# Softmax reciprocal moved from VectorE to GpSimd, with the sum of exponentials placed one product earlier

## Chip, cores and metric

One core of one Trainium2 chip runs the whole kernel. The metric is the device time of one execution in microseconds, the median of several runs. The batch is 8 images of 64 channels and 64 x 64 pixels, in float32.

## What is computed

The reference is an attention layer followed by three residual convolution steps. The attention is unusual: it runs over the batch. For each pixel (4096 of them), the 8 images are the 8 tokens, and 8 heads of 8 channels attend among them. Cut to what matters here:

```
xn = group_norm(x); t = xn @ ciw + pe; tn = layer_norm(t)
q2, k2, v2 = projections of tn, as (image, pixel, head, 8)
scores = einsum('inhd,jnhd->nhij', q2, k2) / sqrt(8)
attn = softmax(scores, axis=-1)          # over the 8 images j
z = einsum('nhij,jnhd->inhd', attn, v2)
t = z @ wout + t;  t = gated_mlp(layer_norm(t), t) + t;  x = t @ cow + x
for _ in range(3): x = x + conv(relu(conv(x, w1) + b1), w2) / 3
out = relu(x)
```

The change touches only the denominator of the softmax.

## The kernel before

**Stages.** `setup_weights` folds the weights and computes the group statistics. `attention_block` walks over 32 tiles (`TILES`) of 128 pixels. `conv_steps` does the convolutions. The change is in `attention_block` alone.

**A tile.** Pixels lie on the 128 partitions. A tile's q, k and v are 64 values per image and pixel. The products q.k of all image pairs and heads are made on VectorE (DVE) as four instructions of 1024 elements per partition each (`dve_p1`, b = 0 to 3, line 516). TensorE (PE) sums them over the 8 channels of a head with eight accumulating transposes for each of the four (line 558), ScalarE (ACT) copies the transposed scores out of PSUM (line 718), and PE transposes them back (line 567). DVE takes the maximum (line 770) and subtracts it (line 781), ACT makes the exponential (line 722), DVE sums over the images into `den`, 128 x 64 (`dve_sum`, line 787), takes the reciprocal into `rden` (`dve_reciprocal`, line 793) and multiplies (`dve_attn`, line 799). Four products attn.v (`dve_p2`, line 526) follow, which PE sums (line 577). Then come the output projection (line 587), the residual `z1` (`dve_z1`, line 813), the second normalization (`tn2`, line 825) and the gated MLP (`gated`, line 839).

**The order of the work.** Each engine has one in-order instruction stream. It is written out by hand in `pe_iteration`, `act_iteration`, `dve_iteration` and `pool_iteration`; iteration t works on up to five tiles at once, t to t - 4. A wait is on a semaphore that another engine's instruction raises; an engine that waits holds back all that stands behind. One iteration of DVE has 21 instructions, among them `sum` of tile t - 2, `var1` of tile t (line 755), `reciprocal` and `attn` of tile t - 2.

**GpSimd (POOL) before the change** has three instructions in an iteration: `pool_rstd2` of tile t - 4, `pool_bias` of tile t - 1 and `pool_rstd1` of tile t. The two `rstd` (lines 900 and 907) take an 8-element variance to the power of -0.5 with a tensor_tensor whose operation is `pow` and whose second operand is a constant tile. `pool_bias` (line 760) adds the q and k biases, 1024 elements per partition. `rstd1` of a tile releases `act_scale` in the next iteration (8 ACTIVATEs, line 713), that releases `pool_bias`, and that the first product `dve_p1(t, 0)`.

```
rstd1 (POOL, iteration t) -> act_scale -> pool_bias (iteration t+1) -> dve_p1 b=0 (end of t+1)
exp (ACT) -> sum -> reciprocal -> attn -> p2 b=0..3 (DVE)
```

Of the kernel before, what the change touches and what calls it, by code (L numbers as in the profile page):

```python
# [12 lines left out]
B, C, HW = 8, 64, 64  # L13
# [7 lines left out]
P = 2 * C  # L21
# [8 lines left out]
ALU, ACT, AX = mybir.AluOpType, mybir.ActivationFunctionType, mybir.AxisListType  # L30
# [4 lines left out]
def wait(eng, sem, n):  # L35

    if isinstance(n, int) and n <= 0:
        return
    eng.wait_ge(sem, n)
# [377 lines left out]
def attention_block(nc, d, top):  # L417


    with ExitStack() as ctx:  # L420
        def sb(name, shape, dt=F32):
            return ctx.enter_context(nc.sbuf_tensor(name, shape, dt))

        def sem(name):
            return ctx.enter_context(nc.semaphore(name))
# [22 lines left out]
        exps = shifted  # L448
        den = sb("den", [P, C])
        rden = sb("rden", [P, C])  # L450
        attn = sb("attn", [P, S])
        z = sb("z", [P, N])
        z1 = [sb(f"z1_{k}", [P, N]) for k in range(2)]
# [30 lines left out]
        den_done, rden_done, biased, p1_dve = sem("den_done"), sem("rden_done"), sem("biased"), sem("p1_dve")  # L484
        p2_dve, tn2_done, var2_done = sem("p2_dve"), sem("tn2_done"), sem("var2_done")
        gated_done, x_done = [sem(f"gated_done{e}") for e in range(2)], [sem(f"x_done{e}") for e in range(2)]
        rstd1_done, rstd2_done, attn_done, rrep_done = sem("rstd1_done"), sem("rstd2_done"), sem("attn_done"), sem("rrep_done")

        ident, center = top["consts"][:, K_ID:K_ID + P], top["consts"][:, K_CEN:K_CEN + P]
# [261 lines left out]
        def dve_var1(dve, t):  # L751
            for g in range(2):
                wait(dve, squares_out[g], t + 1)
            wait(dve, rstd1_done, t)
            dve.tensor_scalar(var1[:, :], sumsq[:, :], 1e-5, None, ALU.add).then_inc(var1_done, 1)  # L755

        def pool_bias(pool, t, k):
            wait(pool, scaled_out, B * (t + 1))
            qk = qkv[k][:, :, 0:2 * C]
            pool.tensor_tensor(qk, qk, top["brep"][:, :].unsqueeze(1).broadcast_to([P, B, 2 * C]), ALU.add).then_inc(biased, 1)  # L760

        def dve_p1(dve, t, k, b):
            wait(dve, biased, t + 1)
            wait(dve, scoresT_mm, DUOS * (t - 1) + b + 1)
            p1_product(dve, k, b).then_inc(p1_dve, 1)

        def dve_max(dve, t):
            wait(dve, scores_mm, t + 1)
            wait(dve, shift_done, t)
            dve.tensor_reduce(smax[:, :].rearrange("p (i h) -> p i h", i=B), scores_view(), AX.X, ALU.max).then_inc(smax_done, 1)  # L770
# [5 lines left out]
        def dve_shift(dve, t):  # L776
            wait(dve, scores_mm, t + 1)
            wait(dve, smax_done, t + 1)
            wait(dve, attn_done, t)
            top_of = smax[:, :].rearrange("p (i h) -> p i h", i=B).unsqueeze(3).broadcast_to([P, B, HEADS, B])  # L780
            dve.tensor_tensor(shifted[:, :].rearrange("p (i h j) -> p i h j", i=B, j=B), scores_view(), top_of, ALU.subtract)\
                .then_inc(shift_done, 1)

        def dve_sum(dve, t):
            wait(dve, exp_out, t + 1)
            wait(dve, rden_done, t)
            dve.tensor_reduce(den[:, :].rearrange("p (i h) -> p i h", i=B),
                              exps[:, :].rearrange("p (i h j) -> p i h j", i=B, j=B), AX.X, ALU.add).then_inc(den_done, 1)

        def dve_reciprocal(dve, t):  # L790
            wait(dve, den_done, t + 1)
            wait(dve, attn_done, t)
            dve.reciprocal(rden[:, :], den[:, :]).then_inc(rden_done, 1)

        def dve_attn(dve, t):
            wait(dve, rden_done, t + 1)
            wait(dve, p2_dve, DUOS * t)
            r = rden[:, :].unsqueeze(2).broadcast_to([P, C, B])
            dve.tensor_tensor(attn[:, :].rearrange("p (g j) -> p g j", j=B),
                              exps[:, :].rearrange("p (g j) -> p g j", j=B), r, ALU.mult).then_inc(attn_done, 1)  # L800

        def dve_p2(dve, t, k, b):
            wait(dve, attn_done, t + 1)
            wait(dve, av_mm, DUOS * (t - 1) + b + 1)
            p2_product(dve, k, b).then_inc(p2_dve, 1)
# [10 lines left out]
        def dve_var2(dve, t):  # L816
            wait(dve, var2_mm, t + 1)
            wait(dve, rstd2_done, t)
            dve.tensor_scalar(var2[:, :], b4[:, 0:B], 1e-5, None, ALU.add).then_inc(var2_done, 1)  # L819
# [9 lines left out]
        def of_half(buffer, e):  # L829

            return buffer[:, :].rearrange("p (d e n) -> p e d n", d=2, e=2)[:, e]

        def dve_gated(dve, t, e):

            wait(dve, a_mm, 2 * t + e + 1)
            for d in range(2):
                wait(dve, gelu_out[d], t + 1)
                wait(dve, out_mm[d], t)
            dve.scalar_tensor_tensor(of_half(gated, e), (b5, b7)[e][:, :].rearrange("p (d n) -> p d n", d=2), cols[:, 2:3],
                                     of_half(gel, e), ALU.add, ALU.mult).then_inc(gated_done[e], 1)  # L840
            if t == TILES - 2 and e == 0:
                outer_ahead(dve, ((0, 0), (0, 1), (1, 0)))
            if t == TILES - 1 and e == 0:
                outer_ahead(dve, ((0, 2), (1, 2)))
# [13 lines left out]
        def dve_x(dve, t, k, d):  # L858

            if isinstance(t, int):  # L860
                dve.wait_ge(xr_in[k % 2], 32 * (t // 2 + 1))
            else:
                dve.wait_ge(xr_in[k % 2], (t - k % 2) * 16 + 32)
            wait(dve, cow_mm, t + 1)
            dve.scalar_tensor_tensor(x_view(t, d), x_psum(d), cols[:, 4:5], xr_view(k, d), ALU.add, ALU.add).then_inc(x_done[d], 1)
# [17 lines left out]
        def outer_ahead(dve, pieces):  # L883
            for i, c in pieces:
                free_for(dve, i)
                written(dve, c)
                mix_outer(dve, top["mixed_x"][i], top["outer_done"][i], c, x_piece(i, c))
# [111 lines left out]
        def dve_iteration(dve, t, k, tiles):  # L999
            if tiles[1]:  # L1000
                dve_p1(dve, t - 1, (k - 1) % RING, 1)
            if tiles[4]:
                dve_gated(dve, t - 4, 1)
                dve_gated(dve, t - 4, 0)
            if tiles[1]:
                dve_p1(dve, t - 1, (k - 1) % RING, 2)
            if tiles[2]:
                dve_sum(dve, t - 2)
            if tiles[0]:
                dve_var1(dve, t)  # L1010
            if tiles[1]:
                dve_p1(dve, t - 1, (k - 1) % RING, 3)
            if tiles[2]:
                dve_reciprocal(dve, t - 2)
                dve_attn(dve, t - 2)
                dve_p2(dve, t - 2, (k - 2) % RING, 0)
            if tiles[3]:
                dve_var2(dve, t - 3)
            if tiles[2]:
                dve_p2(dve, t - 2, (k - 2) % RING, 1)  # L1020
                dve_p2(dve, t - 2, (k - 2) % RING, 2)
            if tiles[4]:
                dve_x(dve, t - 4, (k - 4) % RING, 1)
            if tiles[2]:
                dve_p2(dve, t - 2, (k - 2) % RING, 3)
            if tiles[1]:
                dve_max(dve, t - 1)
                dve_shift(dve, t - 1)
            if tiles[4]:
                dve_x(dve, t - 4, (k - 4) % RING, 0)  # L1030
            if tiles[3]:
                dve_tn2(dve, t - 3)
            if tiles[0]:
                dve_p1(dve, t, k, 0)
            if tiles[2]:
                dve_z1(dve, t - 2, (k - 2) % RING)

        def pool_iteration(pool, t, k, tiles):
            if tiles[4]:
                pool_rstd2(pool, t - 4)  # L1040
            if tiles[1]:
                pool_bias(pool, t - 1, (k - 1) % RING)
            if tiles[0]:
                pool_rstd1(pool, t)

# [6 lines left out]
        def run(eng, iteration):  # L1052

            for t in range(TILES + 5 - 1):
                iteration(eng, t, t % RING, [0 <= t - s < TILES for s in range(5)])
# [3 lines left out]
        @block.tensor  # L1059
        def _(pe):  # L1060
            run(pe, pe_iteration)
# [10 lines left out]

        @block.gpsimd
        def _(pool):
            run(pool, pool_iteration)

        @block.sync
# [451 lines left out]
```

## Time and profile before

| | us |
|---|---|
| median of 3 runs | 1140.54 (1140.28 to 1140.69) |
| span of the profiled execution | 1136.3 |
| PE busy | 1071.2 (94%) |
| DVE busy | 1039.7 (92%) |
| ACT busy | 652.5 (57%) |
| POOL busy | 510.7 (45%) |

The run of the profile has no time of its own apart from its span; the span counts from the first to the last instruction and lies 4.2 us under the median of the runs. Setup ends at about 44.6 us, the attention pipeline is full from about 95 to 565 us and drains until about 600 us, and the rest is convolution. PE's ends are modelled, so 94% does not say that PE is at its peak.

### The profile page before, as it was taken

What the parts mean: (1) busy time and instruction counts of PE and PEld (TensorE: products, weight loads), DVE (VectorE), ACT (ScalarE), POOL (GpSimd) and SP (SyncE); (2) the same over time, 40 slices, a digit from 0 to 9 for tenths busy, and PEclk for the clock granted to TensorE, in tenths of its full rate; (3) what the DMA queues carried; (4) which work ended last, traced back from release to release, by engine and by line L of the source; (5) the groups of instructions that cost most, each with busy time, mean ns of one, the idle gap of its engine ahead of it and who ended that gap; (6) DMA issues with size and microseconds to landing.
All of it is one profiled execution on the core that took longest, in us unless ns stands there. A gap on an engine that the chain in (4) does not pass through costs nothing. (4 is left out here: it accounts for less than half of the span.)

```text
span 1136.3 us, 21019 instructions
## 1 busy us (share of the span) xinstructions
PE 1071.2 (94%) x7238; PEld 601.7 (53%) x7238; DVE 1039.7 (92%) x1475; ACT 652.5 (57%) x1525; POOL 510.7 (45%) x422
## 2 busy tenths in 40 slices
PE   4269999999999999999999999999999999999996
PEld 3156787778777777777653333333333333333331
DVE  5459999999999999999988999999999999999996
ACT  4568889888888888888743233253244242342333
POOL 5134564456445544554452424435345344444440
PEclk9999999999999999999999999999999999999998
DMA  8110111111111111110000000030001100030003
GB/s 303 54 37 21 39 29 35 32 39 29 33 35 38 29 31 38 38 29 20 20 20 1 1 1 1 1 75 1 1 1 34 41 1 1 1 74 1 1 1 74
DMA packets 87545, 35.83 MB, mean 32 GB/s; under 512 B 70210, under 2 KB 86851, under 8 KB 86931
## 3 DMA queue, kind: packets, MB, share of 16 engines
q1 hardware_dynamic: 85634, 33.81, 11.1%
q8 instruction: 61, 1.00, 0.4%
q0 software_dynamic: 768, 0.33, 0.2%
q10 hardware_dynamic: 1040, 0.35, 0.1%
q14 instruction: 42, 0.34, 0.1%
HBM read 26.09 MB, written 8.39 MB: 30 GB/s over the span
## 5 line engine op out<-in xcount | busy, mean ns | idle before, releaser
L1173 ACT ACTIVATE y<-banks,cols 128x1024 f32<-128x1024 f32 x96 | 110.3, 1208 | 259.8 <-PE banks L1165 259.8
L900 POOL TENSOR_TENSOR rstd<-var,half 128x8 f32<-128x8 f32 x32 | 80.8, 2526 | 216.5 <-DVE var L755 216.5
L1155 PE MATMUL banks<-mixed_h,cwp 128*128 128x512 f32 x384 | 177.6, 605 | 0.0
L1155 PE MATMUL banks<-early,cwp 128*128 128x512 f32 x372 | 169.2, 602 | 0.5 <-PEq L420 0.5
L1456 POOL TENSOR_TENSOR early<-xs 128x256 f32<-128x256 f32 x95 | 77.1, 811 | 160.1 <-DVE xs L1204 160.1
L1181 DVE TENSOR_TENSOR y<-y,banks 128x512 f32<-128x512 f32 x192 | 119.9, 682 | 15.2 <-ACT y L1173 15.0
L558 PE MATMUL banks<-consts,early 128*128 128x128 f32 x1024 | 133.2, 279 | 0.0
L1189 DVE TENSOR_TENSOR y<-y,banks 128x512 f32<-128x512 f32 x192 | 124.4, 685 | 8.7 <-PE banks L1165 6.5
L577 PE MATMUL banks<-consts,prod 128*128 128x128 f32 x1024 | 128.2, 273 | 2.8 <-DVE prod L526 2.1
L1155 PEld LDWEIGHTS banks<-mixed_h,cwp 128*128 128x128 f32 x384 | 69.0, 189 | 107.9 <-issue 107.9
L558 PEld LDWEIGHTS banks<-consts,early 128*128 128x128 f32 x1024 | 114.3, 144 | 18.8 <-issue 18.1
L516 DVE TENSOR_TENSOR early<-early 128x1024 f32<-128x1024 f32 x96 | 116.6, 1219 | 7.4 <-POOL early L760 7.1
L1155 PEld LDWEIGHTS banks<-early,cwp 128*128 128x128 f32 x372 | 67.7, 190 | 101.4 <-issue 88.8
L526 DVE TENSOR_TENSOR prod<-attn,early 128x1024 f32<-128x1024 f32 x96 | 116.7, 1241 | 0.8
L577 PEld LDWEIGHTS banks<-consts,prod 128*128 128x128 f32 x1024 | 114.6, 141 | 4.5 <-DVE prod L526 3.4
L1196 ACT ACTIVATE h<-y 128x512 f32<-128x512 f32 x96 | 55.0, 625 | 90.2 <-DVE y L1189 89.3
L907 POOL TENSOR_TENSOR rstd<-var,half 128x8 f32<-128x8 f32 x32 | 80.6, 2520 | 53.7 <-DVE var L819 53.7
L1456 POOL TENSOR_TENSOR mixed_h<-h 128x256 f32<-128x256 f32 x48 | 37.5, 781 | 127.4 <-ACT h L1196 127.4
L1165 PE MATMUL banks<-mixed_h,cwp 64*64 64x512 f32 x768 | 93.5, 602 | 0.0
L1165 PE MATMUL banks<-early,cwp 64*64 64x512 f32 x768 | 90.7, 598 | 0.0
L547 PE MATMUL banks<-basis,tt 64*128 64x256 f32 x512 | 76.4, 418 | 11.3 <-ACT tt L688 5.9
L1449 DVE TENSOR_TENSOR early<-xs 128x512 f32<-128x512 f32 x96 | 83.7, 912 | 0.8
(184 smaller groups left out, 1868.8 us busy)
## 6 DMA issues: line engine op xcount, KB each, us to landing
xs<-in_x SPq DMA_DIRECT2D x4, 2048.0 KB, 16.5
xa<-in_x SPq DMA_DIRECT2D x32, 256.0 KB, 2.8
xr<-in_x SPq DMA_DIRECT2D x64, 128.0 KB, 2.8
out_y<-xs SPq DMA_DIRECT2D x32, 256.0 KB, 4.5
cw<-in_L_conv_w POOLq DMA_DIRECT2D x2, 144.0 KB, 3.9
consts<-in_consts ACTq DMA_DIRECT2D x1, 192.0 KB
group<-in_consts SPq DMA_DIRECT2D x1, 64.0 KB
w1n<-in_L_conv_w ACTq DMA_DIRECT2D x1, 64.0 KB
```

What stands on the lines that cost most here:

```text
L516: return eng.tensor_tensor(out, q, kk, ALU.mult)
L526: return eng.tensor_tensor(out, a, v, ALU.mult)
L558: m = pe.matmul(b2[:, P * b:P * (b + 1)], prod1[:, e, P * b:P * (b + 1)], ident, start=(e == 0), stop=(e == HD - 1), is_transpose=True)
L577: m = pe.matmul(b4[:, TILE * p:TILE * (p + 1)], prod2[:, j, P * p:P * (p + 1)], ident, start=(j == 0 and p == 0), stop=(j == B - 1 and p = ...
L900: pool.tensor_tensor(rstd1[:, :], var1[:, :], top["half"][:, :], ALU.pow).then_inc(rstd1_done, 1)
L1155: pe.matmul(psum[PSUM_PAIR[v, q, j]][i][:, :, :], weights(v, i, j).rearrange("p n o -> p (n o)"), mixed[v][i][:, s0:s0 + WIDE, j, :], star ...
L1165: m = pe.matmul(psum[PSUM_PAIR[v, q, j]][i][out, :, :], edge_weights(v, i, j)[rows, :], mixed[v][i][rows, s0 + near:s0 + near + WIDE, j, : ...
L1173: act.activation(pairs(y[i][q][:, :, :]), m1, ACT.Identity, bias=cols[:, (6, 8)[v]:(7, 9)[v]]).then_inc(m1_out[i][q], 1)
L1181: m = dve.tensor_tensor(even_odd, even_odd, psum[PSUM_PAIR[v, q, 3]][i][:, :, :], op)
L1189: dve.tensor_tensor(even_odd, even_odd, psum[PSUM_PAIR[v, q, j]][i][:, :, :], ALU.add).then_inc(y_done[i][q][j], 1)
L1449: eng.tensor_tensor(r, column_pairs(x[:, :, 0:HW]), column_pairs(x[:, :, 2:2 + HW]), ALU.subtract).then_inc(done[c], 1)
L1456: eng.tensor_tensor(r[:, :, 2, :], even_odd[:, 0], even_odd[:, 1], ALU.add)
```

## The change

`reciprocal` leaves DVE. POOL makes the same value as `den` to the power of -1 with a tensor_tensor of 64 elements per partition, against a constant tile `minus` filled once with -1.0. The new instruction stands in POOL's order between `pool_bias` and `pool_rstd1`. On DVE `sum` moves ahead of the third product, so that the third product (b = 2), `var1` and the fourth product (b = 3) stand between `sum` and `attn`.

```diff
+        minus = sb("minus", [P, C])
...
-        def dve_reciprocal(dve, t):
-            wait(dve, den_done, t + 1)
-            wait(dve, attn_done, t)
-            dve.reciprocal(rden[:, :], den[:, :]).then_inc(rden_done, 1)
+        def pool_reciprocal(pool, t):
+            wait(pool, den_done, t + 1)
+            wait(pool, attn_done, t)
+            if t == 0:
+                wait(pool, minus_set, 1)
+            pool.tensor_tensor(rden[:, :], den[:, :], minus[:, :], ALU.pow).then_inc(rden_done, 1)
...
+            if tiles[2]:
+                dve_sum(dve, t - 2)
             if tiles[1]:
                 dve_p1(dve, t - 1, (k - 1) % RING, 2)
-            if tiles[2]:
-                dve_sum(dve, t - 2)
             if tiles[0]:
                 dve_var1(dve, t)
             if tiles[1]:
                 dve_p1(dve, t - 1, (k - 1) % RING, 3)
             if tiles[2]:
-                dve_reciprocal(dve, t - 2)
                 dve_attn(dve, t - 2)
...
             if tiles[1]:
                 pool_bias(pool, t - 1, (k - 1) % RING)
+            if tiles[2]:
+                pool_reciprocal(pool, t - 2)
             if tiles[0]:
                 pool_rstd1(pool, t)
...
+            pool.memset(minus[:, :], -1.0).then_inc(minus_set, 1)
```

DVE's order in the middle of an iteration in the kernel before (early is the buffer of the q.k products, qkv a ring buffer of q, k and v):

```order
L516 TENSOR_TENSOR early<-qkv 128x16x8x8
L787 TENSOR_REDUCE den<-shifted 128x64
L755 TENSOR_SCALAR var<-sumsq 128x8
L516 TENSOR_TENSOR early<-qkv 128x16x8x8
L793 RECIPROCAL rden<-den 128x64
L799 TENSOR_TENSOR attn<-shifted,rden 128x512
L526 TENSOR_TENSOR prod<-attn,early 128x1024
```

The same place with the change, where the line numbers are a few higher:

```order
L789 TENSOR_REDUCE den<-shifted 128x64
L518 TENSOR_TENSOR early<-qkv 128x16x8x8
L757 TENSOR_SCALAR var<-sumsq 128x8
L518 TENSOR_TENSOR early<-qkv 128x16x8x8
L803 TENSOR_TENSOR attn<-shifted,rden 128x512
L528 TENSOR_TENSOR prod<-attn,early 128x1024
```

`den` is ready one product earlier, and DVE has one instruction fewer per iteration. POOL's order before, one and a half iterations:

```order
L760 TENSOR_TENSOR qkv<-qkv,brep 128x8x128
L900 TENSOR_TENSOR rstd<-var,half 128x8
L907 TENSOR_TENSOR rstd<-var,half 128x8
L760 TENSOR_TENSOR early<-early,brep 128x8x128
L900 TENSOR_TENSOR rstd<-var,half 128x8
```

And with the change, with what each waits for:

```order
L762 TENSOR_TENSOR qkv<-qkv,brep 128x8x128 [waits scaled_out]
L797 TENSOR_TENSOR rden<-den,minus 128x64 [waits attn_done,den_done]
L904 TENSOR_TENSOR rstd<-var,half 128x8 [waits scaled_out,var1_done]
L911 TENSOR_TENSOR rstd<-var,half 128x8 [waits rrep_done,var2_done]
L762 TENSOR_TENSOR early<-early,brep 128x8x128 [waits scaled_out]
```

`rstd1` (L900, now L904) and everything behind it on POOL now stands behind the 64-element `pow`.

## Rows read from the trace of the kernel before

**Rows 1.** Busy time by stretch, whole core; the row of the full attention pipeline.
```profile
core 0: us, PE busy (x) PEld busy (x) DVE busy (x) ACT busy (x) POOL busy (x), PEclk, DMA share, GB/s
95.00:565.00 470.00, 468.39 (x4362) 355.77 (x4361) 457.40 (x607) 408.75 (x1140) 246.28 (x87) 1.00 0.13 32
```

**Rows 2.** Timeline, one iteration of DVE: start, duration, engine, line.
```profile
300.13 1.22 DVE L516 TENSOR_TENSOR early<-qkv 128x1024 f32<-128x1024 f32 x1
301.62 0.75 DVE L813 SCALAR_TENSOR_TENSOR z<-banks,cols,tt 128x512 f32<-128x512 f32 x1 [0.27 <-PE banks L587]
...
304.74 1.22 DVE L516 TENSOR_TENSOR early<-qkv 128x1024 f32<-128x1024 f32 x1
305.87 0.68 DVE L787 TENSOR_REDUCE den<-shifted 128x64 f32<-128x512 f32 x1
306.47 0.17 DVE L755 TENSOR_SCALAR var<-sumsq 128x8 f32<-128x8 f32 x1
306.57 1.23 DVE L516 TENSOR_TENSOR early<-qkv 128x1024 f32<-128x1024 f32 x1
307.71 0.55 DVE L793 RECIPROCAL rden<-den 128x64 f32<-128x64 f32 x1
308.29 0.69 DVE L799 TENSOR_TENSOR attn<-shifted,rden 128x512 f32<-128x512 f32 x1
309.02 1.22 DVE L526 TENSOR_TENSOR prod<-attn,early 128x1024 f32<-128x1024 f32 x1
310.24 2.35 DVE L526 TENSOR_TENSOR prod<-attn,early 128x1024 f32<-128x1024 f32 x2
314.04 0.68 DVE L770 TENSOR_REDUCE smax<-banks 128x64 f32<-128x512 f32 x1
316.41 1.22 DVE L516 TENSOR_TENSOR early<-early 128x1024 f32<-128x1024 f32 x1
```

**Rows 3.** Timeline of POOL in the same iteration.
```profile
306.71 2.58 POOL L900 TENSOR_TENSOR rstd<-var,half 128x8 f32<-128x8 f32 x1 [6.64 <-DVE var L755]
310.40 2.55 POOL L907 TENSOR_TENSOR rstd<-var,half 128x8 f32<-128x8 f32 x1 [1.10 <-DVE var L819]
312.92 3.44 POOL L760 TENSOR_TENSOR early<-early,brep 128x1024 f32<-128x1024 f32 x1
```

**Rows 4.** POOL's power instructions of 4 and 8 elements while DVE holds nothing up.
```profile
40.66 1.04 POOL L346 TENSOR_TENSOR ga<-gvar,gexp 128x4 f32<-128x4 f32 x1 [9.59 <-DVE gvar L296]
...
54.10 1.64 POOL L900 TENSOR_TENSOR rstd<-var,half 128x8 f32<-128x8 f32 x1 [12.40 <-DVE var L755]
...
209.03 1.65 POOL L900 TENSOR_TENSOR rstd<-var,half 128x8 f32<-128x8 f32 x1 [6.64 <-DVE var L755]
```

**Rows 5.** Timeline of DVE beside the last of them.
```profile
209.24 1.23 DVE L516 TENSOR_TENSOR early<-early 128x1024 f32<-128x1024 f32 x1 [0.28 <-issue]
```

**Rows 6.** A GpSimd add with reads of 1024 elements, between attn.v products, pipeline filling.
```profile
81.87 6.79 DVE L526 TENSOR_TENSOR prod<-attn,early 128x1024 f32<-128x1024 f32 x4
...
85.15 2.43 POOL L760 TENSOR_TENSOR early<-early,brep 128x1024 f32<-128x1024 f32 x1 [2.99 <-ACT early L713]
```

**Rows 7.** ACT and PE behind `rstd1`, same iteration as rows 2 and 3.
```profile
309.33 2.88 ACT L713 ACTIVATE early<-early,rstd 128x192 f32<-128x192 f32 x8 [0.26 <-POOL rstd L900]
...
312.12 0.57 ACT L718 ACTIVATE scoresT<-banks 128x512 f32<-128x512 f32 x1
...
313.39 0.60 PE L567 MATMUL banks<-consts,scoresT 128*128 128x128 f32 x4
```

**Rows 8.** PE in the full pipeline, and while the pipeline fills with PE mostly idle.
```profile
299.82 1.14 PE L547 MATMUL banks<-basis,tt 64*128 64x256 f32 x8
...
59.80 2.08 PE L547 MATMUL banks<-basis,tt 64*128 64x256 f32 x8 [4.08 <-ACT tt L688]
63.69 2.08 PE L547 MATMUL banks<-basis,tt 64*128 64x256 f32 x8 [1.81 <-ACT early L705]
65.70 4.37 PE L558 MATMUL banks<-consts,early 128*128 128x128 f32 x24
70.00 0.67 PE L535 MATMUL banks<-xa,resT 64*64 64x128 f32 x16
70.60 1.09 PE L558 MATMUL banks<-consts,early 128*128 128x128 f32 x8
...
44.60:70.00 25.40, 14.54 (x88) 10.46 (x84) 5.45 (x7) 11.88 (x53) 6.55 (x3) 1.00 0.07 22
```

**Rows 9.** Timeline of PE behind `sum`, same iteration as rows 2.
```profile
306.07 1.97 PE L558 MATMUL banks<-consts,early 128*128 128x128 f32 x16
307.87 0.95 PE L613 MATMUL banks<-consts,sq 128*128 128x2 f32 x8
308.69 1.07 PE L558 MATMUL banks<-consts,early 128*128 128x128 f32 x8
309.69 0.66 PE L677 MATMUL banks<-z,cowT 64*64 64x256 f32 x8
310.17 0.62 PE L535 MATMUL banks<-xa,resT 64*64 64x128 f32 x16
```

More of the change, by code:

```diff
@@ L486, in attention_block @@
         gated_done, x_done = [sem(f"gated_done{e}") for e in range(2)], [sem(f"x_done{e}") for e in range(2)]
+        minus_set = sem("minus_set")
         rstd1_done, rstd2_done, attn_done, rrep_done = sem("rstd1_done"), sem("rstd2_done"), sem("attn_done"), sem("rrep_done")
```

## The prediction

> **What bounds the kernel now.** I read the busy times by stretch first. While the attention pipeline is full, PE is busy for 468 of 470 us and DVE for 457 [rows 1]. Both look saturated, so the next view is the timeline of one iteration. DVE's iteration has no hole but one, 0.27 us ahead of `z1`, which waits for PE [rows 2]. The product of the next iteration starts at 316.41, the one before at 300.13: the period is 16.28 us. DVE sets it; PE is close behind. POOL has room: its three instructions take 2.58, 2.55 and 3.44 us [rows 3], 8.57 of 16.28, and it idles 6.64 us before `rstd1`.
>
> I cut DVE's period at two points. `sum` ends at 305.87 + 0.68 = 306.55, and `attn` starts at 308.29: 1.74 us. From `attn` to the next first product is 316.41 - 308.29 = 8.12 us. From that product to the end of the next `sum` is 16.28 - 1.74 - 8.12 = 6.42 us.
>
> **What leaves DVE.** The reciprocal goes, and `attn` would come 308.29 - 307.71 = 0.58 us earlier [rows 2]. If nothing else changed, 32 iterations would save 18.6 us.
>
> **What moves.** One product (305.87 - 304.74 = 1.13 us) moves from ahead of `sum` to behind it. The stretch from the first product to the end of `sum` falls to 6.42 - 1.13 = 5.29 us. Between `sum` and `attn` DVE then has two products and `var1`, about 1.05 + 0.10 + 1.14 = 2.3 us after the end of `sum`. PE gets the third product 0.6 us later, which is covered: PE has later products queued behind it.
>
> **What POOL gains: the price of 64 powers.** This is the term that decides. The trace has three instructions that stand alone: a power of 4 elements per partition took 1.04 us, one of 8 elements 1.64 and 1.65 us [rows 4]. So four more elements cost 0.60 us, 0.15 us each, on a base of 1.04 - 0.60 = 0.44. Continued to 64 elements this is 0.44 + 64 x 0.15 = 10.0 us. The ends: if the 4-element one, the first power of the program, contains something that happens once, the slope is steeper, at most 1.64 / 8 = 0.205 us per element, 13.1 us. At the other end stands the add of 1024 elements in 2.43 us [rows 6]: were a power as quick per element, 64 of them would cost little more than 8 do, at least 1.65 us. I take 10.0, since both nearest rows are powers and the add is another operation.
>
> The Trainium skill (GPSIMD Engine Reference, section 3.1) gives a GpSimd tensor_tensor about 2.6 cycles per element at 1.2 GHz, which is 2.2 ns, without setting power apart. By that rule 64 elements cost 0.14 us over the fixed part, and the change would win; the trace agrees with the page for the add (2.43 us for 1024 elements) and not for the power.
>
> **The shared read path.** In the full pipeline the 8-element power takes 2.58 us, 0.93 more than 1.65. It starts 0.14 us into a DVE product with two SBUF inputs, and ends 0.93 later, about the rest of that product [rows 2, 3]. In the one iteration where it started first (209.03 against 209.24) it took 1.65, and the DVE product came late by 0.28 [rows 4, 5]. The reverse holds too: four DVE products took 6.79 us instead of 4.6 with an add of POOL in between [rows 6]. So whoever starts first reads first. The new power starts 0.07 us after `sum` ends (as `rstd1` does after `var1`, 306.64 to 306.71), when the third product has run for 0.15 us: add 0.93. Then POOL reads, and the fourth product probably waits until its reads are nearly through. That product should end near the end of the power; if it comes wholly behind, it costs 1.1 us more. I take 0.
>
> **`sum` to `attn`**: 0.07 + 0.93 + 10.04 + 0.04 = 11.08 us, in place of 1.74. The cover of 2.3 us is much too short.
>
> **What stands behind it.** `rstd1` now starts when the power ends, so level with `attn` and no longer 1.58 us before it. It then runs without a DVE product in its way, 1.65 us; the eight scalings start there and are followed by the score copy 2.79 us on (309.33 to 312.12), 0.57 long, then 0.60 of PE [rows 7]: 1.60 + 2.79 + 0.57 + 0.04 + 0.60 + 0.05 = 5.65 us after `attn`. `max` starts 314.04 - 308.29 = 5.75 after it today. So this chain just fits. `bias` can start at 1.60 + 2.88 + 0.1 = 4.6 after `attn`, today 312.92 - 308.29 = 4.63. The 8.12 us stay. A delay of `rstd1` of 0.9 by the read path would show in full.
>
> **PE.** Behind `sum` it has the transposes of three products, `var2`'s, and lines 677 and 535 to do, 1.97 + 0.95 + 1.07 + 0.66 + 0.62 = 5.3 us from about the end of `sum` [rows 9]. What comes next in its order needs the fourth product, and then attn.v products, the first of which ends at 11.08 + 1.95 = 13.0. Between 5.3 and 13.0 PE has one group of eight transposes. While the pipeline filled, 8 matmuls of line 547 took 2.08 us, against 1.14 in the full one; the group after the idle time of 4.08 us was slow, and PE was quick again by 70.00, after 63.69 to 70.00 of unbroken work [rows 8]. That is the pace of 1.2 against 2.4 GHz, though the granted clock is given as 1.00 there. At the slow pace the transposes behind `attn` take about 1.6 us per eight instead of 0.9: the first sixteen run from 2.0 to 5.2, the scores to 6.1, and `max` starts at about 6.4 instead of 5.75. Between 0 (the pace stays) and 4 us (slow all the way to `z1`), I take 0.7: PE gets back to speed within the burst.
>
> The Trainium skill (TensorE: Matmul & The Clock Gate, Part 1) says that an idle TensorE is gated to half its clock and gets it back after sustained work. The rows agree by the doubled durations; that it will happen in this gap no row here shows.
>
> **Sum.** Period 11.08 + 8.12 + 5.29 + 0.7 = 25.2 us, 8.9 more than 16.28. All 32 tiles have one such reciprocal, and DVE goes from `sum` to `attn` in each, in the filling and draining iterations too: 32 x 8.9 = 285 us. The sum stands against the profiled execution, 1136.3 + 285 = 1421; with the 4.2 us around the span, 1425 us. The memset at the start and the semaphore cost nothing: POOL waits 12.40 us before its first `rstd1` [rows 4]. The convolutions are untouched.
>
> **The rivals.**
> - **Steeper price.** The power costs in proportion, 13.1 us. For: the first power may hold a one-time cost that flattens my slope. Against: 54.10 and 209.03 agree within 0.01, so no such cost shows elsewhere. The period rises by 3.1 more, 99 us in all: 1524. Chance 0.2.
> - **Gentler price.** A loop with a long start makes the slope from 4 to 8 elements larger than further on; halfway, 5 to 8 us. The period is then 2 to 5 us shorter than forecast, 1265 to 1360. Chance 0.15.
> - **The power hides: faster.** The price of 64 elements is nearly that of 8, if a power ran at the pace of the add, 2.43 us for 1024 elements [rows 6]. With 1.65 + 0.93 it ends 2.65 after `sum`; the period is 2.69 + 8.12 + 5.29 = 16.10, 6 us saved: 1135. With a power below about 1.3 us the two products are the limit, 18.6 saved: 1122. The point from which it decides: `sum` to `attn` must stay below 16.28 - 8.12 - 5.29 = 2.87 us, so the power, with its 0.93 of waiting, below 2.76, or 1.83 alone. That is 0.19 more than 8 elements take. Chance 0.04. (The rule of the Trainium skill's GPSIMD Engine Reference, quoted above, would give this case.)
> - **It does not do what it says**: since POOL runs in order, the power could start late because `bias` stands ahead of it. `bias` ends at 316.36, the next `sum` at 306.55 + 16.28 = 322.8: it does not bind. Chance below 0.01.
>
> **How the numbers follow.** The forecast has 0.6 for powers of about 9 to 11 us, with or without the slow pace of PE: 1403 without it (285 less 22), 1460 if the fourth product falls wholly behind as well. The range reaches from the upper half of the gentler price to the steeper: 1320 to 1530. A measurement can tell 0.2%, 2.3 us, from no change. Faster by more: 0.04, from the rival of that name. Within: 0.01, the narrow strip around the break-even. Slower: 0.95.
>
> **What would show it.** The POOL row of line 797 with a mean of 10 to 11.5 us. DVE idle before `attn` (line 803), 7 to 9 us per tile, released by POOL `rden`. POOL's busy share above DVE's in the attention. PE's groups of line 547 or 577 slower than 1.14 and 0.9 us if the clock falls. `rstd1` at 1.65 us, since no product stands in its way. Wrong would be a mean of line 797 below 3 us, or a period between two `attn` other than 24 to 26.5 us with that mean at 10.

## The result, and the profile after

The changed kernel takes 1453.4 us (median of 4 runs, 1452.5 to 1454.1) against 1140.4 us before: the ratio is 1.2747, with a 95% interval of 1.2729 to 1.2765. That is 313 us more, 9.8 us per tile. The forecast was 1425.

The page of the changed kernel, its span and busy times:

```profile
span 1452.0 us, 21021 instructions
...
PE 1148.7 (79%) x7238; PEld 672.9 (46%) x7238; DVE 1029.4 (71%) x1443; ACT 648.8 (45%) x1525; POOL 850.6 (59%) x455
```

Every engine except POOL has a smaller share of a longer span. POOL is at 59% and no bound by its share. The groups of instructions say who waits (busy and mean of one, then idle time ahead of them and its releaser):

```profile
L797 POOL TENSOR_TENSOR rden<-den,minus 128x64 f32<-128x64 f32 x32 | 366.1, 11441 | 202.9 <-DVE den L789 202.9
L579 PE MATMUL banks<-consts,prod 128*128 128x128 f32 x1024 | 190.8, 358 | 237.1 <-DVE var L823 230.7
L803 DVE TENSOR_TENSOR attn<-shifted,rden 128x512 f32<-128x512 f32 x32 | 22.1, 692 | 292.5 <-POOL rden L797 292.5
```

The power takes 11.44 us. POOL waits for `den`, DVE waits for `rden`: two engines take turns, 292.5 us of DVE standing in all, 9.1 us per tile. PE stands behind both.

One iteration in the timeline, DVE and POOL, to be held against [rows 2, 3]:

```profile
400.31 1.64 POOL L904 TENSOR_TENSOR rstd<-var,half 128x8 f32<-128x8 f32 x1
400.38 0.69 DVE L803 TENSOR_TENSOR attn<-shifted,rden 128x512 f32<-128x512 f32 x1 [9.12 <-POOL rden L797]
...
409.78 1.22 DVE L518 TENSOR_TENSOR early<-early 128x1024 f32<-128x1024 f32 x1
...
411.74 0.75 DVE L817 SCALAR_TENSOR_TENSOR z<-banks,cols,tt 128x512 f32<-128x512 f32 x1 [0.74 <-PE banks L589]
...
414.86 0.67 DVE L789 TENSOR_REDUCE den<-shifted 128x64 f32<-128x512 f32 x1
...
415.45 1.22 DVE L518 TENSOR_TENSOR early<-early 128x1024 f32<-128x1024 f32 x1
...
415.61 11.47 POOL L797 TENSOR_TENSOR rden<-den,minus 128x64 f32<-128x64 f32 x1 [7.17 <-DVE den L789]
416.78 1.21 DVE L518 TENSOR_TENSOR early<-early 128x1024 f32<-128x1024 f32 x1
...
427.11 0.69 DVE L803 TENSOR_TENSOR attn<-shifted,rden 128x512 f32<-128x512 f32 x1 [9.12 <-POOL rden L797]
```

From the end of `sum` (415.53) to `attn` (427.11) it is 11.58 us; from `attn` to the next first product 9.40 us (8.12 before); from there to the end of `sum` 5.75 us. This iteration is one of the longer ones, 26.73. The periods lie between 25.1 and 26.7; the starts of the power at 129.80 and 856.07, 28 periods apart, give a mean of 25.94 us. 32 times the 9.66 us over 16.28 are 309 of the 313 us. The rest is in filling and draining.

PE in the same iteration, and its granted clock in two stretches (start and end, length, busy PE, PEld, DVE, ACT, POOL, then PEclk):

```profile
402.48 3.66 PE L579 MATMUL banks<-consts,prod 128*128 128x128 f32 x16 [7.28 <-DVE var L823]
...
406.78 1.91 PE L579 MATMUL banks<-consts,prod 128*128 128x128 f32 x8
...
408.97 1.04 PE L579 MATMUL banks<-consts,prod 128*128 128x128 f32 x8
```

```profile
402.40:408.90 6.50, 6.42 (x32) 6.44 (x33) 5.58 (x8) 5.05 (x15) 5.95 (x2) 0.52 0.01 3
408.90:421.00 12.10, 12.10 (x116) 8.19 (x114) 8.08 (x10) 8.61 (x25) 5.39 (x1) 1.00 0.10 24
```

After 7.28 us of standing, eight transposes take 1.9 us, and 1.04 later. The granted clock says the same: 0.52 for the 6.5 us behind `attn`, that is 1.2 GHz nearly throughout, and 1.00 after it. Here the record shows what the filling pipeline of the kernel before showed by durations only [rows 8].

### The profile page after: what moved, and what is told of

It is laid out like the page before. It is cut to its first block and busy times, and to the rows that moved or that the text cites. A ratio compares the mean times of both kernels' runs of the same rounds, so it can differ in the third digit from the quotient of the medians.

```text
span 1452.0 us, 21021 instructions
## 1 busy us (share of the span) xinstructions
PE 1148.7 (79%) x7238; PEld 672.9 (46%) x7238; DVE 1029.4 (71%) x1443; ACT 648.8 (45%) x1525; POOL 850.6 (59%) x455
## 5 line engine op out<-in xcount | busy, mean ns | idle before, releaser
L797 POOL TENSOR_TENSOR rden<-den,minus 128x64 f32<-128x64 f32 x32 | 366.1, 11441 | 202.9 <-DVE den L789 202.9
L579 PE MATMUL banks<-consts,prod 128*128 128x128 f32 x1024 | 190.8, 358 | 237.1 <-DVE var L823 230.7
L579 PEld LDWEIGHTS banks<-consts,prod 128*128 128x128 f32 x1024 | 173.4, 193 | 244.4 <-DVE var L823 237.8
L803 DVE TENSOR_TENSOR attn<-shifted,rden 128x512 f32<-128x512 f32 x32 | 22.1, 692 | 292.5 <-POOL rden L797 292.5
L715 ACT ACTIVATE early<-early,rstd 128x192 f32<-128x192 f32 x192 | 69.1, 442 | 214.2 <-POOL rstd L904 214.2
L911 POOL TENSOR_TENSOR rstd<-var,half 128x8 f32<-128x8 f32 x32 | 80.7, 2522 | 23.8 <-DVE var L823 23.8
```

The lines of the kernel that those rows point to most:

```text
L579: m = pe.matmul(b4[:, TILE * p:TILE * (p + 1)], prod2[:, j, P * p:P * (p + 1)], ident, start=(j == 0 and p == 0), stop=(j == B - 1 and p = ...
L797: pool.tensor_tensor(rden[:, :], den[:, :], minus[:, :], ALU.pow).then_inc(rden_done, 1)
L911: pool.tensor_tensor(rstd2[:, :], var2[:, :], top["half"][:, :], ALU.pow).then_inc(rstd2_done, 1)
```

## Experiments

**The price of the power, by itself.** Eight unneeded instructions on constant tiles, while DVE has next to nothing to do.

```diff
+            for width, power, op in ((4, 1, ALU.pow), (8, 1, ALU.pow), (16, 1, ALU.pow), (32, 1, ALU.pow),
+                                     (64, 1, ALU.pow), (64, 2, ALU.pow), (8, 2, ALU.pow), (64, 1, ALU.mult)):
+                pool.tensor_tensor(probe[3][:, 0:width], probe[0][:, 0:width], probe[power][:, 0:width], op)
```

> The kernel before, with eight more GpSimd instructions on constant tiles at the start of the attention block, each waiting for the one before: powers of 4, 8, 16, 32 and 64 elements with exponent -1, of 64 and 8 elements with exponent -0.5, and a product of 64 elements. VectorE does nothing meanwhile. Theory (price linear, 0.44 + 0.15 per element, the rest of the 11.44 us seen in the changed kernel is waiting for VectorE's reads): 1.04, 1.64, 2.85, 5.25, 10.0 us, the same for -0.5, and 0.2 us for the product. Rival (the price alone is 11.4, the read path costs the 64-element power nothing): 64 elements at 11.4. The total rises by about 25 us since GpSimd's first needed instruction comes later; that number decides nothing.

Groups of instructions by shape:

```profile
L1083 POOL TENSOR_TENSOR probe<-probe 128x64 f32<-128x64 f32 x3 | 21.4, 7135 | 0.2
L1083 POOL TENSOR_TENSOR probe<-probe 128x32 f32<-128x32 f32 x1 | 5.4, 5426 | 0.1
L1083 POOL TENSOR_TENSOR probe<-probe 128x8 f32<-128x8 f32 x2 | 3.3, 1635 | 0.2
L1083 POOL TENSOR_TENSOR probe<-probe 128x16 f32<-128x16 f32 x1 | 2.9, 2898 | 0.1
...
L1083 POOL TENSOR_TENSOR probe<-probe 128x4 f32<-128x4 f32 x1 | 1.0, 1011 | 0.1
```

and the two powers of 64 elements, exponents -1 and -0.5, from the timeline:

```profile
56.26 10.54 POOL L1083 TENSOR_TENSOR probe<-probe 128x64 f32<-128x64 f32 x1
...
66.88 10.54 POOL L1083 TENSOR_TENSOR probe<-probe 128x64 f32<-128x64 f32 x1
```

The group of three 128x64 holds those two and the product, 3 x 7.135 - 2 x 10.54 = 0.32 us. From 32 to 64 elements the slope is (10.54 - 5.43) / 32 = 0.160 us per element, from 8 to 32 it is 0.158. The price is linear, 0.37 + 0.159 per element, and the exponent does not matter. The rest of 11.44 is 0.90 us of waiting for DVE's third product, against 0.93 in the forecast. The changed kernel says the same: the power of its last tile, with no such product beside it, took 10.55 us. The run took 1165 us; that number decides nothing.

**Half the elements.** POOL takes 32 columns, DVE the other 32, in its own idle time.

```diff
-            pool.tensor_tensor(rden[:, :], den[:, :], minus[:, :], ALU.pow).then_inc(rden_done, 1)
+            pool.tensor_tensor(rden[:, 0:32], den[:, 0:32], minus[:, 0:32], ALU.pow).then_inc(rden_done, 1)
...
+        def dve_rest(dve, t):
...
+            dve.reciprocal(rden[:, 32:C], den[:, 32:C]).then_inc(rest_done, 1)
```

> The changed kernel with the power on the first 32 of 64 columns and VectorE's reciprocal on the other 32, placed right ahead of attn, where VectorE waits anyway. Theory (the period is the power's time plus what lies around it): the power falls from 11.44 to about 6.3 us, the mean period from 25.9 to 20.8; TensorE then stands for about 2.5 us less than 8 and should keep its clock, which gives back up to 1.7 more: 1235 to 1290. Rival (something else than the power's length sets the period, such as the order on GpSimd): above 1350.

1277.9 us, ratio 1.1211 (1.1194 to 1.1227). Timeline of POOL:

```profile
301.47 6.35 POOL L798 TENSOR_TENSOR rden<-den,minus 128x32 f32<-128x32 f32 x1 [6.03 <-DVE den L790]
...
321.95 6.35 POOL L798 TENSOR_TENSOR rden<-den,minus 128x32 f32<-128x32 f32 x1 [6.02 <-DVE den L790]
```

The power fell by 5.1 us and the period, 321.95 - 301.47 = 20.48, by 5.5. So the length of the power sets the period. One part of the expectation was wrong: the clock was not kept. PE stands for only 2.17 us here and still does the next transposes slowly:

```profile
309.95 3.08 PE L579 MATMUL banks<-consts,prod 128*128 128x128 f32 x16 [2.17 <-DVE var L830]
```

```profile
309.90:313.90 4.00, 3.95 (x21) 3.46 (x22) 3.77 (x4) 4.00 (x13) 3.94 (x2) 0.61 0.02 4
```

The granted clock is 0.61 in that stretch. The time lies in the expected range all the same.

**TensorE kept busy.** The changed kernel with 56 unneeded transposes where PE would stand.

```diff
             if tiles[3]:
+                wait(pe, gelu_out[1], t - 3)
+                for _ in range(56):
+                    pe.transpose(b3[:, 0:P], ident, ident)
                 pe_av(pe, t - 3, 0)
```

> The changed kernel with 56 unneeded transposes of a constant on TensorE, per tile, where it stands and waits for the first attn.v product; they write to a part of a bank that is overwritten before it is read. Theory (part of the mean period of 25.9 us is TensorE working at 1.2 GHz after its idle time): the granted clock stays at 1.00, the transposes behind attn take 0.9 us per eight, attn to the next first product falls from 9.4 to about 8.1 us, z1's wait from 0.74 to under 0.3; 1.4 to 1.8 us per tile, 1396 to 1409. Rival (TensorE is late because of its order or of its waits and not by its clock): no gain, 1453 or more.

1424.2 us, ratio 1.2495 (1.2474 to 1.2516), 29 us less than the changed kernel. The full pipeline, then one iteration of DVE:

```profile
95.00:850.00 755.00, 692.06 (x6210) 554.14 (x6208) 465.76 (x600) 417.42 (x1176) 569.66 (x119) 1.00 0.08 21
```

```profile
414.07 0.69 DVE L803 TENSOR_TENSOR attn<-shifted,rden 128x512 f32<-128x512 f32 x1 [9.11 <-POOL rden L797]
...
422.18 1.22 DVE L518 TENSOR_TENSOR early<-qkv 128x1024 f32<-128x1024 f32 x1
```

The clock stays at 1.00 (0.83 in the same stage without the transposes), `attn` to the first product is 8.11 us, and the period is 24.95: 0.99 us less. So the slow clock is shown as the cause of this part of the loss, and its size is 1.0 us per tile on average. The 1.4 to 1.8 expected, 1396 to 1409 us, was too much: it came from one of the long iterations. How much is lost goes with how soon within the burst the clock comes back. In a short iteration of the changed kernel, 25.13 us from the `attn` at 349.06 to the next, it is back after 2.8 us:

```profile
351.20:354.00 2.80, 2.80 (x14) 2.80 (x15) 2.80 (x4) 2.80 (x9) 2.80 (x2) 0.51 0.00 0
354.00:357.70 3.70, 3.70 (x34) 3.49 (x34) 3.56 (x6) 2.71 (x8) 3.13 (x1) 1.00 0.00 0
```

**The power off the chain.** The kernel before, reciprocal on DVE, with an unneeded power on POOL for which nobody waits.

```diff
             if tiles[1]:
                 pool_bias(pool, t - 1, (k - 1) % RING)
+            if tiles[2]:
+                pool_spare(pool, t - 2)
...
+            pool.tensor_tensor(spare[2][:, :], spare[0][:, :], spare[1][:, :], ALU.pow)
```

> The kernel before, reciprocal on VectorE, plus one unneeded power of 64 elements per tile on GpSimd, between bias and rstd1, on constant tiles, waited for by nobody. It asks whether the power could be hidden by moving its use further away. Theory (GpSimd's own work becomes the limit): GpSimd must fit 10.54 + 2 x 1.65 to 2.55 + 2.4 to 3.4 = 16.3 to 19.1 us into 16.28, and its bias waits for the scalings behind rstd1; a period of 17.5 to 19.5 us, 1180 to 1245. Rival (only the chain sum, power, attn costs, GpSimd has room): 1140 to 1150.

1205.2 us, ratio 1.0577 (1.0559 to 1.0594). POOL has almost no idle time left:

```profile
293.67 10.55 POOL L802 TENSOR_TENSOR spare<-spare 128x64 f32<-128x64 f32 x1
304.19 2.28 POOL L909 TENSOR_TENSOR rstd<-var,half 128x8 f32<-128x8 f32 x1
306.44 2.37 POOL L916 TENSOR_TENSOR rstd<-var,half 128x8 f32<-128x8 f32 x1
309.46 2.37 POOL L762 TENSOR_TENSOR early<-early,brep 128x1024 f32<-128x1024 f32 x1 [0.64 <-ACT early L715]
311.79 10.55 POOL L802 TENSOR_TENSOR spare<-spare 128x64 f32<-128x64 f32 x1
```

The period is 18.12 us. So 1.84 us per tile, 65 us of run time in all, are lost with this power in this place on POOL even when nobody needs its result, since POOL's own work no longer fits. This is a floor and not a share of the 313 us: in the changed kernel the period of 25.94 us lies above these 18.12, and the chain `sum`, power, `attn` sets it. Even if the result could be used late enough to hide the power wholly, at most 248 of the 313 us would come back, and 65 would stay.

**The second half of the change alone.** `sum` ahead of the third product, reciprocal on DVE.

```diff
+            if tiles[2]:
+                dve_sum(dve, t - 2)
             if tiles[1]:
                 dve_p1(dve, t - 1, (k - 1) % RING, 2)
-            if tiles[2]:
-                dve_sum(dve, t - 2)
```

> The kernel before with the sum moved ahead of the third q.k product and the reciprocal left on VectorE: the second half of the change alone. Theory (VectorE is saturated, order within it is free): 1140, within 0.2%. Rival (the third product 0.6 us later holds up TensorE, which is nearly as busy): up to 0.6 us per tile, 1160.

1139.0 us, ratio 0.9995 (0.9986 to 1.0005). No difference, as expected.

**The change at a price of nothing.** A product in place of the power.

```diff
-            pool.tensor_tensor(rden[:, :], den[:, :], minus[:, :], ALU.pow).then_inc(rden_done, 1)
+            pool.tensor_tensor(rden[:, :], den[:, :], minus[:, :], ALU.mult).then_inc(rden_done, 1)
```

> The changed kernel with a product in place of the power, of the same shape, engine, place and waits: the reciprocal is left out of the computation. It shows the change at a price of 0.2 us in place of 10. Theory (all of the loss is the price of the power): VectorE loses 0.58 us per tile and nothing else moves, 1140.4 - 18.6 = 1122. Rival 1 (the place behind the bias and ahead of rstd1, or the extra hop between engines, costs by itself): 1140 or more. Rival 2 (TensorE is the limit once VectorE has 0.58 us less): 1125 to 1137.

1144.4 us, ratio 1.0035 (1.0022 to 1.0049). This was the surprise: the loss of 313 us is gone, but so is the gain of 18.6. DVE has 0.58 us less to do and the period is exactly the old one. The start of PE's line 631 in two iterations:

```profile
299.96 1.13 PE L631 MATMUL banks<-tn,w1T 64*128 64x512 f32 x4
...
316.24 1.13 PE L631 MATMUL banks<-tn,w1T 64*128 64x512 f32 x4
```

It is 16.28 us, and between these two PE has no idle time. DVE spends most of what it saved on a second wait for PE:

```profile
312.51 0.69 DVE L772 TENSOR_REDUCE smax<-banks 128x64 f32<-128x512 f32 x1 [0.40 <-PE banks L569]
```

and, as before, 0.28 us ahead of `z1`.

**Relieving TensorE, alone and together.** The kernel before, and the one with the product, each with six instead of eight transposes per score sum.

```diff
-            for e in range(HD):
+            for e in range(HD - 2):
                 m = pe.matmul(b2[:, P * b:P * (b + 1)], prod1[:, e, P * b:P * (b + 1)], ident,
-                              start=(e == 0), stop=(e == HD - 1), is_transpose=True)
+                              start=(e == 0), stop=(e == HD - 3), is_transpose=True)
```

> The kernel before with 6 accumulating transposes in place of 8 in each of the four score sums: two of the eight channels of a head are left out of the scores. TensorE has 8 transposes, about 0.87 us, less per tile; VectorE's work is the same. Theory A (VectorE sets 16.28 us, with its one hole of 0.27): at most 0.27 per tile, 1131 to 1140. Theory B (TensorE alone sets it and VectorE only looks full because it is paced): 15.4 us, 1113. Both together bound it: 1131.

> The same cut of two channels together with the product in place of the power on GpSimd, so that the reciprocal is left out as well: both engines are relieved. The product alone left the period at 16.28 us and gave 1144. Theory (TensorE's instructions fill 16.28 us by themselves and VectorE's come to some 16.0, so either relief alone gives at most 0.3): both together 15.4 to 15.7 us, 1144 less 19 to 28: 1116 to 1126. Rival (a chain over GpSimd and ScalarE, rstd1 to bias, holds the 16.28): 1140 to 1144.

| DVE's reciprocal | PE's transposes | us | ratio to before (95%) | period, us |
|---|---|---|---|---|
| as before | 8 per sum | 1140 | 1 | 16.28 |
| gone | 8 | 1144.4 | 1.0035 (1.0022 to 1.0049) | 16.28 |
| as before | 6 | 1128.3 | 0.9898 (0.9883 to 0.9913) | 15.88 |
| gone | 6 | 1130.8 | 0.9918 (0.9904 to 0.9933) | 15.78 |

With PE alone relieved, the time, 1128.3 us, lies between what the two theories gave, and DVE's timeline has no hole at all in a period of 15.88 us:

```profile
302.99 0.54 DVE L793 RECIPROCAL rden<-den 128x64 f32<-128x64 f32 x1
...
318.87 0.54 DVE L793 RECIPROCAL rden<-den 128x64 f32<-128x64 f32 x1
```

So DVE's own work is 15.88 us and PE's 16.28: PE set the period before, by 0.40 us, and DVE only looked as if it did. Taking the reciprocal away pays nothing with PE unrelieved, and 0.10 us per tile with PE relieved. That is less than expected (15.4 to 15.7 us, 1116 to 1126). DVE saves 0.58 us there and still takes 15.78, so neither its own work nor PE's sets this period. The trace shows what does. These are the rows of the loop alone, from one `var1` of DVE to the next:

```profile
237.48 0.29 DVE L757 TENSOR_SCALAR var<-sumsq 128x8 f32<-128x8 f32 x1
237.85 2.55 POOL L904 TENSOR_TENSOR rstd<-var,half 128x8 f32<-128x8 f32 x1
240.43 2.88 ACT L715 ACTIVATE early<-early,rstd 128x192 f32<-128x192 f32 x8 [0.34 <-POOL rstd L904]
243.22 0.57 ACT L720 ACTIVATE scoresT<-banks 128x512 f32<-128x512 f32 x1
243.85 0.66 PE L569 MATMUL banks<-consts,scoresT 128*128 128x128 f32 x4 [0.16 <-ACT scoresT L720]
...
248.41 0.75 DVE L817 SCALAR_TENSOR_TENSOR z<-banks,cols,tt 128x512 f32<-128x512 f32 x1 [0.27 <-PE banks L589]
...
253.25 0.28 DVE L757 TENSOR_SCALAR var<-sumsq 128x8 f32<-128x8 f32 x1
```

Each of these starts as the one before it ends, PE works without a hole from its line 569 to the output projection that `z1` waits for, and DVE from `z1` to the next `var1`. So a loop over four engines closes in 15.77 us: `var1`, `rstd1`, the scalings, the score copy, PE, `z1`. It is akin to the rival that the expectation named, a chain over GpSimd and ScalarE, though it goes through the score copy and not `bias`, and holds 15.78 and not 16.28. This is read from the trace; no run shortened a link of the loop. This kernel also carries the loss of the next section, which is why it takes longer than the one with VectorE's reciprocal in spite of its shorter period.

**Where the last 4 us went.** The kernel with the product is 4 us slower than before at the same period. It started the last `rstd1` 1.4 us earlier (549.51 against 550.91), so it lost about 6 in draining. In that stage POOL makes the first pieces for the convolution; with the change they stand behind the last tile's reciprocal. The last tile got DVE's reciprocal back:

```diff
-            if tiles[2]:
+            if tiles[2] and t - 2 < TILES - 1:
                 pool_reciprocal(pool, t - 2)
...
+            if t == TILES - 1:
+                dve_last(dve, t)
...
+            dve.reciprocal(rden[:, :], den[:, :]).then_inc(rden_done, 1)
```

> The kernel with the product on GpSimd, but with VectorE's reciprocal in the last of the 32 tiles, so that GpSimd has nothing of that tile ahead of the first pieces of the convolution (the reciprocal is left out of the other 31 tiles). Theory (the kernel with the product lost about 6 us in the draining of the pipeline, since GpSimd's pieces for the convolution came 6 us later behind the last tile's product, collided with attn.v products, and let TensorE go slow): 1137 to 1140. Rival (the loss lies elsewhere): 1144.

1137.9 us, ratio 0.9986 (0.9977 to 0.9995). Draining, with the product on POOL (L1463 is a piece for the convolution, 579.42 a product of the last tile):

```profile
578.34 0.32 POOL L797 TENSOR_TENSOR rden<-den,minus 128x64 f32<-128x64 f32 x1 [7.74 <-DVE den L789]
578.60 0.31 POOL L898 MEMSET early<- 128x256 f32 x1
...
579.42 1.52 DVE L528 TENSOR_TENSOR prod<-attn,qkv 128x1024 f32<-128x1024 f32 x1
579.82 1.59 POOL L1463 TENSOR_TENSOR early<-xs 128x256 f32<-128x256 f32 x1
```

and with the last tile on DVE:

```profile
570.50 0.30 POOL L905 MEMSET early<- 128x256 f32 x1
```

The pieces come 8 us earlier, do not meet the attn.v products of the last tile, and `rstd2` behind them comes 3.7 us earlier (580.76 against 584.49). The granted clock of 565 to 605 us is 1.00; in the other it was 0.92 from 565 to 609. The 6 us are settled. So two things had to come together to give 1144.4: PE is the limit in the full pipeline, and POOL's new place costs in draining. In this last kernel, where the reciprocal costs DVE nothing in 31 tiles and POOL 1.23 us (0.32 alone, the rest is waiting at its start), the whole gain is 0.14%: that is about what the idea could have brought.

## Why the prediction was right

**The power's price** was the deciding term and held: 10.54 us measured against 10.04, with the linear law from two rows of 4 and 8 elements. The term was undersized by 0.50 because the slope is 0.159 and not 0.150. **The wait on the read path** was right at 0.90 against 0.93. **`sum` to `attn`**: 11.58 against 11.08, all of the difference from the price. DVE's idle time ahead of `attn`, 9.1 us, lies just above the 7 to 9 forecast. The rivals with a steeper and a gentler price fall.

**What stands behind it** was right: with the clock kept, 8.11 us from `attn` to the first product against 8.12, and `rstd1` runs in 1.64.

**PE's clock** was right in kind, and undersized: 0.99 against 0.7 us. The transposes take 1.9 us per eight and not the 1.6 assumed. Together, 0.50 + 0.29 is nearly the 0.74 us by which the mean period, 25.94, exceeds the 25.2 forecast. Over 32 tiles that is 24 of the 28 us missing from the forecast. The rest is in the draining, which the forecast took to cost no more than the one reciprocal: from the start of the last `attn` to the end it is 1452.0 - 890.9 = 561.1 us, against 1136.3 - 580.8 = 555.5 before, 5.6 more. The last power stands ahead of the first convolution pieces there, as the product does, and a piece takes 1.59 us, as it did behind the product:

```profile
880.32 10.55 POOL L797 TENSOR_TENSOR rden<-den,minus 128x64 f32<-128x64 f32 x1 [8.08 <-DVE den L789]
...
892.03 1.59 POOL L1463 TENSOR_TENSOR early<-xs 128x256 f32<-128x256 f32 x1
```

That their place is the cause was tried with the product only.

**One expectation on the fourth product was wrong.** It was to wait until POOL had nearly read everything; it started 0.2 us after the start of `var1` (416.78) and ran its usual 1.21 us beside the power. So the running power did not keep this product out. This cost nothing, as I had taken 0.

**One step of the reading failed: "DVE sets it; PE is close behind"**, and with it the 18.6 us under "what leaves DVE" and the time of the faster rival, 1122. PE sets it at 16.28, and DVE needs 15.88: taking transposes from PE shortened the period, taking the reciprocal from DVE did not. The sign was in [rows 2]: DVE's only hole, 0.27 us, was a wait for PE, while PE was busy for 468.4 of 470 us [rows 1]. An engine that waits in every iteration for another one that never waits is not the one that sets the period, however small its wait. The forecast did not suffer since the long wait was a different chain, but the best case of the change was about 2 us, not 19. For the same reason the point given for break-even, a power of 1.83 us alone, should be no break-even between gain and loss but the end of a stretch without effect; no run was made near it.

## What to carry to other kernels

Price an operation by its own rows at two sizes, and extend the line: an add of 1024 elements and a power of 8 took the same 2.4 to 2.6 us in this kernel and said nothing about each other. Before moving work off a full engine, look for its waits: if it waits for a second full engine in every iteration, the relief is worth what that one allows. And an in-order engine that takes on a dependent instruction also takes all that stands behind it into the chain, in the draining of the pipeline too.

## What the runs showed of the hardware

- A GpSimd power of float32 costs 0.37 us and 0.159 us per element per partition, 4 to 64 elements, at exponents -1 and -0.5; a product of 64 elements 0.32 us. VectorE's reciprocal of 64 took 0.55 us.
- TensorE's granted clock was 0.52 in the 6.5 us behind 7.28 us of standing, and 0.61 in the 4 us behind 2.17 us of standing in the kernel with 32 elements. In the changed kernel it was 1.00 again 2.8 us after TensorE took up work in one iteration, and 6.4 us after it in another. With 56 unneeded transposes in place of most of the standing it stayed at 1.00.
- A DVE product beside a running GpSimd power was not delayed (1.21 us), while the power waited 0.9 us at its start for one already running. `var1` beside the power took 0.29 us, against 0.17 in the kernel before. Two GpSimd adds beside DVE products do slow these: a product beside them took 1.52 us in place of 1.22 (draining, kernel with the product on GpSimd).
